# A feed-forward stage rebuilt: one batch through all eight experts, three batches by their two experts in 19 sorted tiles

## The chip, the core and the metric

The kernel runs on one core of a Trainium2 chip. The metric is the device time of one execution in microseconds. Five engines work beside each other, each on a list of its own: TensorE (PE in the profile, its weight loads PEld), VectorE (DVE), ScalarE (ACT), GpSimd (POOL) and SyncE (SP). SyncE here only starts transfers; ScalarE and GpSimd can start them too. An engine waits for another by a semaphore, and what stands behind a waiting instruction on its engine waits with it.

## The reference

Four batches of 256 tokens with 128 features. First cross-attention to 1,601 keys a batch, then a mixture of eight experts, of which each token uses two.

```python
x = x + attention(layernorm(x), ctx, Wq, bq, Wk, bk, Wv, bv)
h = layernorm(x).reshape(1024, 128)
scores = softmax(h @ router_weight.T + router_bias)          # 8 experts
topk_w, topk_idx = top_k(scores, 2)
gu = einsum('th,ehn->ten', h, gate_up_proj) + gate_up_bias   # 8 x (128 -> 512)
gate, up = minimum(gu[..., :256], 7), clip(gu[..., 256:], -7, 7)
act = (up + 1) * gate * sigmoid(1.702 * gate)
down = einsum('tei,eih->teh', act, down_proj) + down_bias    # 8 x (256 -> 128)
x = x + (down[topk_idx] * topk_w).sum(axis=1)
```

All is float32. Products whose rounding would move the result are made of three matmuls in a faster format: each operand is split into a high and a low part, and high x high, high x low and low x high are summed (`three`, lines 941 to 946).

## The kernel before

The 1,024 tokens are eight tiles of 128 (two a batch). The attention handles one tile after another: scores against 1,601 keys in four chunks (12 matmuls), clipping and maximum on VectorE, one exponential over the row on ScalarE (L419), 13 transposes of the probabilities (L1025), 13 matmuls with the context (L1041). TensorE's list interleaves tile n+1's scores with tile n's transposes and sums. At the end of each batch come the value projection (L1054), the residual (L655), the second layer norm (L662 to L674, its inverse root on GpSimd, L287), the transposes of the normalised tokens (L1064) and the router (8 logits a token).

The feed-forward stage computes all eight experts for all tokens and weighs the results; the six experts that a token doesn't use have weight zero. It has 16 steps: a step is one expert for one half (512 tokens), in the order (expert 0, half 0), (1, 0), (0, 1), (1, 1), then the next pair of experts. In a step TensorE computes four banks of 128 hidden units by 512 tokens, three matmuls of 512 columns each (`gate_up`), and after that the down projection of an earlier step, 16 matmuls of 128 columns (`down`, L1147). ScalarE applies silu and relu with bias to the banks (L498, L504) and scales the down results by the router's weights (L524); VectorE clips and multiplies (L838, L847) and splits the weights of each expert in high and low (L774, L779); GpSimd adds a step's result to the residual (L350). The steps of experts 2 to 5 stand in a loop, the rest is written out. All hands off in fixed order by semaphores; there is no planner.

The expert weights lie in SBUF as one tensor, loaded once. What the tokens are routed to changes only the weights of the sum, never which work is done or where it is read from. Results go out in three transfers, the first half while the last steps run.

## Time and profile before

| | |
|---|---|
| median of 3 runs | 156.98 us (156.92 to 156.98) |
| the profiled execution | 156.96 us, of which 155.2 us from the first to the last instruction |
| TensorE's granted clock | 1.00 of full speed (2.4 GHz) in every slice |
| busy: TensorE, VectorE, ScalarE, GpSimd | 96%, 66%, 65%, 32% |
| attention, up to the last tile's sums | 0 to 74.5 us, with the first steps of the experts in its end |
| feed-forward alone | 75.8 to 152.5 us on TensorE |
| after the last matmul | 2.7 us |

A line of the profile names engine, line, operation, output<-inputs and size; "busy" is the time in which such instructions ran, and the mean is of one. Two matmuls in a row overlap: one of 395 ns starts 234 ns after the one before it. So what a row of matmuls costs is read from the starts, not from the means. The same holds for ScalarE where nothing is waited for.

### The profile page before, as it was taken

What the parts mean: (1) busy time and instruction counts of PE and PEld (TensorE: products, weight loads), DVE (VectorE), ACT (ScalarE), POOL (GpSimd) and SP (SyncE); (2) the same over time, 40 slices, a digit from 0 to 9 for tenths busy, and PEclk for the clock granted to TensorE, in tenths of its full rate; (3) what the DMA queues carried; (4) which work ended last, traced back from release to release, by engine and by line L of the source; (5) the groups of instructions that cost most, each with busy time, mean ns of one, the idle gap of its engine ahead of it and who ended that gap; (6) DMA issues with size and microseconds to landing.
All of it is one profiled execution on the core that took longest, in us unless ns stands there. A gap on an engine that the chain in (4) does not pass through costs nothing.

```text
span 155.2 us, 3023 instructions
## 1 busy us (share of the span) xinstructions
PE 149.2 (96%) x1004; PEld 136.0 (88%) x1004; DVE 103.2 (66%) x288; ACT 100.8 (65%) x205; POOL 49.8 (32%) x49
## 2 busy tenths in 40 slices
PE   7998799999999999999999999999999999999993
PEld 7988699999999999989988888788888888887892
DVE  0668958386859595963683899957654377552773
ACT  3183878657484736468866656957788677779450
POOL 1356529243505300210067643312333321233020
PEclk9999999999999999999999999999999999999999
DMA  4979999700000000000000000000000000000022
GB/s 116 371 292 404 388 401 384 225 1 4 0 2 0 4 0 0 4 0 2 0 0 4 0 0 0 0 4 0 2 0 0 0 0 0 0 4 0 4 68 68
DMA packets 5909, 10.69 MB, mean 69 GB/s; under 512 B 380, under 2 KB 3080, under 8 KB 5896
## 3 DMA queue, kind: packets, MB, share of 16 engines
q1 hardware_dynamic: 4968, 10.00, 17.9%
q10 hardware_dynamic: 928, 0.53, 1.2%
...
q14 instruction: 6, 0.05, 0.1%
HBM read 10.00 MB, written 0.52 MB: 68 GB/s over the span
## 4 chain that ended last, share of the span: by engine, by line
PE 78%; DVE 10%; POOL 4%; ACT 3%; issue 3%; DVEq 0%
PE T L1147 14%; PE O L1041 13%; PE S L944 11%; PE S L946 10%; PE S L945 10%; PE T L1025 6%; PE S L951 3%; POOL ex L309 2%; DVE xT L847 2%; DVE up L838 1%; PE S L1147 1%; DVE w_lo L779 1%; DVE sc L631 1%; ACT pr L419 1%; POOL rstd L287 1%
## 5 line engine op out<-in xcount | busy, mean ns | idle before, releaser
L838 DVE TENSOR_SCALAR up<-up 128x512 f32<-128x512 f32 x32 | 13.9, 434 | 24.7 <-ACT up L504 24.7
L350 POOL TENSOR_TENSOR x<-x,xn 128x512 f32<-128x512 f32 x13 | 17.3, 1331 | 38.6 <-ACT xn L524 38.6
L427 ACT ACTIVATE pT<-T 128x512 f32<-128x512 f32 (+1 forms) x32 | 15.4, 513 | 18.4 <-PE T L1025 18.4
L524 ACT ACTIVATE xn<-T,w_scaled 128x128 f32<-128x128 f32 x56 | 16.1, 374 | 17.2 <-PE T L1147 14.1
L944 PE MATMUL S<-x_hi,w_hi 128*128 128x512 f32 x64 | 26.8, 419 | 0.2 <-DVE w_lo L779 0.2
L1041 PE MATMUL O<-pT,ctx_sb 128*128 128x128 f32 (+1 forms) x208 | 25.9, 275 | 0.2 <-ACT pT L427 0.2
L945 PE MATMUL S<-x_lo,w_hi 128*128 128x512 f32 x64 | 25.3, 395 | 0.0
L946 PE MATMUL S<-x_hi,w_lo 128*128 128x512 f32 x64 | 25.3, 395 | 0.0
L1041 PEld LDWEIGHTS O<-pT,ctx_sb 128*128 128x128 f32 (+1 forms) x208 | 24.6, 192 | 0.6 <-ACT pT L427 0.5
L631 DVE TENSOR_SCALAR_CACHE_REDUCE sc<-S,clip_hi 128x400 f32<-128x400 f32 (+1 forms) x32 | 18.9, 630 | 8.7 <-PE S L946 8.5
L498 ACT ACTIVATE keysT_sb<-S,gate_bias 128x512 f32<-128x512 f32 x32 | 22.7, 708 | 1.7 <-PE S L946 1.6
L504 ACT ACTIVATE up<-S,up_bias 128x512 f32<-128x512 f32 x32 | 22.5, 704 | 0.0
L287 POOL TENSOR_TENSOR rstd<-ve,minus_half 128x2 f32<-128x2 f32 (+1 forms) x7 | 7.5, 1076 | 36.7 <-DVE ve L674 27.6
L317 POOL TENSOR_TENSOR ct_lo<-keysT_sb,ct_hi 128x400 fp32r<-128x400 f32 (+1 forms) x12 | 12.5, 1060 | 14.0 <-ACT ct_hi L410 14.0
L1147 PEld LDWEIGHTS T<-dn_sb,xT 128*128 128x128 f32 x128 | 15.4, 192 | 0.9 <-issue 0.4
L1147 PE MATMUL T<-dn_sb,xT 128*128 128x128 f32 (+1 forms) x128 | 15.8, 276 | 0.2 <-DVE xT L847 0.2
L1025 PE MATMUL T<-ident,pr 128*128 128x128 f32 (+1 forms) x104 | 15.1, 274 | 0.6 <-ACT pr L419 0.6
L946 PEld LDWEIGHTS S<-x_hi,w_lo 128*128 128x128 f32 x64 | 12.0, 188 | 3.0
L1147 PEld LDWEIGHTS T<-dn_sb,act_odd 128*128 128x128 f32 x112 | 13.6, 191 | 1.0 <-DVE act_odd L847 0.4
L944 PEld LDWEIGHTS S<-x_hi,w_hi 128*128 128x128 f32 x64 | 12.1, 189 | 2.5 <-DVE w_lo L779 0.4
L1147 PE MATMUL T<-dn_sb,act_odd 128*128 (+1 forms) x112 | 14.0, 277 | 0.2 <-DVE act_odd L847 0.2
L945 PEld LDWEIGHTS S<-x_lo,w_hi 128*128 128x128 f32 x64 | 12.1, 189 | 2.1
(127 smaller groups left out, 248.4 us busy)
## 6 DMA issues: line engine op xcount, KB each, us to landing
...
ctx_sb<-in_ctx SPq DMA_DIRECT2D x3, 256.0 KB, 4.5
...
out_x<-xn SPq DMA_DIRECT2D x1, 256.0 KB, 2.3
out_x<-xn SPq DMA_DIRECT2D x2, 128.0 KB, 1.8
```

The source lines that it names most:

```text
L350: nc.gpsimd.tensor_tensor(acc, acc, y_sb[:, k % 2, :], ALU.add).then_inc(y_added, 1)
L498: nc.scalar.activation(gate[:, k % 2, ih, :], S[2 * ih][:], ACT.Silu, bias=gate_bias[:, bass.ds(col + ih, 1)], scale=ALPHA).then_inc(silu_ ...
L504: nc.scalar.activation(up[:, k % 2, ih, :], S[2 * ih + 1][:], ACT.Relu, bias=up_bias[:, bass.ds(col + 2 + ih, 1)]).then_inc(up_ready, 1)
L524: ins = nc.scalar.activation(y_sb[:, k % 2, t * DIM:(t + 1) * DIM], T[k % 2][:, t * DIM:(t + 1) * DIM], ACT.Copy, scale=w_scaled[:, bass.d ...
L631: nc.vector.tensor_scalar(sc[:, n % 2, c0:c0 + w], S[c][:, 0:w], clip_hi[:, n:n + 1], None, ALU.min, ALU.max, accum_out=row_max[:, n, c:c ...
L838: nc.vector.tensor_scalar(up[:, k % 2, ih, :], up[:, k % 2, ih, :], 2.0 * LIMIT, 1.0 - LIMIT, ALU.min, ALU.add).then_inc(up_clipped, 1)
L944: nc.tensor.matmul(dst, a_hi, b_hi, start=True, stop=False)
L945: nc.tensor.matmul(dst, a_hi, b_lo, start=False, stop=False)
L946: return nc.tensor.matmul(dst, a_lo, b_hi, start=False, stop=True)
L1025: ins = nc.tensor.transpose(T[bank][0:rows, (t - t0) * P:(t - t0 + 1) * P], pr[:, n % 2, t * P:t * P + rows], ident[:])
L1041: ins = nc.tensor.matmul(O[:, q * P:(q + 1) * P], ctx_sb[b][0:rows, t, :], pT[0:rows, t, :], start=(t == 0), stop=(t == KT - 1))
L1147: ins = nc.tensor.matmul(dst, act_t[k % 2][:, ih, t * P:(t + 1) * P], dn_sb[:, bass.ds((e * 2 + ih) * DIM, DIM)], start=(ih == 0), stop=(i ...
```

## The change

The attention stays. The feed-forward stage is another one:

- **Routing decides the work.** Batch 1 is still computed densely, all eight experts for its 256 tokens, in 16 dense steps of 128 hidden units (`dense_gate_up`, `dense_down`). Its work stands between the last attention tile and the first sorted tile.
- The 768 tokens of batches 0, 2 and 3 are sorted by expert. Each token's normalised row is copied twice (`copy_payload`), with its place in the result as 129th column. From the ranks of the logits VectorE finds the two experts; small matmuls (`count_before`) count how many rows go before each one; GpSimd computes the row numbers (`find_rows`) and scatters the rows by twelve indirect transfers of 128 rows (`send_rows`) into `slot_rows` in HBM, which one transfer of 3.6 MB has filled with ones before.
- VectorE computes a table of 19 tiles (12 full ones, and up to 7 more since each expert starts on a tile of its own): first row and expert of each. SyncE reads the first row of each tile from SBUF into a register and loads the tile from HBM. TensorE reads all 19 expert numbers into registers, in a row, after its first tile's transpose.
- A sorted tile is 128 rows of one expert: a transpose, a split, four matmuls of 512 columns (the bias by a matmul of its own, then three with the weights at the register's place), silu on ScalarE, clip and product on VectorE, two transposes, two matmuls of the down projection, and one indirect transfer from GpSimd that scatters the 128 results to `token_results` in HBM.
- When all 19 are there, they are loaded (256 KB a batch), weighed and added by VectorE, and sent out.
- All weights are split during the attention, in high parts by ScalarE (8 of 128x512) and low parts by GpSimd (6) and VectorE (2); they arrive in three transfers, in the space of the transposed keys.

The core of the diff:

```diff
+                e0, n = W_PARTS[k]
+                sp.wait_ge(keys_lo_ready, (k + 1) * NCH)
+                sp.dma_start(keysT_sb[:, k, 0:n * 2 * HIDDEN].rearrange("p (e n) -> p e n", e=n),
+                             gu[e0:e0 + n].rearrange("e h n -> h e n")).then_inc(w_in[k], 16)
...
+            def load_slots(i):
+                at = sp.value_load(first_row[0:1, i:i + 1], min_val=0, max_val=ROWS - P)
+                sp.dma_start(xt[:, i, :], xs[bass.ds(at, P), :]).then_inc(xt_in[i], 16)
...
+            sp.wait_ge(first_row_ready, 1)
+            for s in range(len(SPARSE)):
+                sp.wait_ge(rows_sent[s], 16 * TOP_K * TPB)
+            for i in range(SLOTS):
+                load_slots(i)
...
+            for place_of, count in sends():
+                sp.wait_ge(y_sent[place_of], count)
+            for s in (0, 2):
+                sp.dma_start(yb_sb[:, s], yb_v[:, s]).then_inc(yc_in[s], 16)
...
+            def send_rows(s, choices=range(TOP_K)):
+                pool.wait_ge(pads_in, 16)
...
+                for c in choices:
+                    for t in range(TPB):
+                        k = c * TPB + t
+                        nc.gpsimd.indirect_dma_start(xs[:, :], bass.IndirectOffsetOnAxis(ap=row_of[:, s, k:k + 1], axis=0),
+                                                     xp[:, SPARSE[s], c, t, :], None, bounds_check=ROWS - 1,
+                                                     oob_is_err=False).then_inc(rows_sent[s], 16)
+            def send_result(i):
+                pool.wait_ge(y_ready, i + 1)
+                nc.gpsimd.indirect_dma_start(yb[:, :], bass.IndirectOffsetOnAxis(ap=xt[:, i, DEST:DEST + 1].bitcast(I32), axis=0),
+                                             y_sb[:, i % Y_RING, :], None, bounds_check=TOP_K * RTOK - 1,
...
             root2(1)
+            weights_lo(3)
+            weights_lo(5)
+            find_rows(0)
+            send_rows(0, [0])
+            weights_lo(6)
+            weights_lo(7)
             root2(2)
+            copy_payload(2)
+            send_rows(0, [1])
+            find_rows(1)
...
+            send_rows(1)
+            copy_payload(3)
+            find_rows(2)
+            send_rows(2)
+            router_exponentials(3)
+            for i in range(SLOTS):
+                send_result(i)
+                if i < EXPERTS:
+                    add_dense(i)
...
-            def silus(step, k, col, ih):
-                act.wait_ge(gu_done, step * 4 + 2 * ih + 1)
-                if not isinstance(step, int) or step >= 2:
-                    act.wait_ge(act_ready, step * 2 + ih - 3)
-                nc.scalar.activation(gate[:, k % 2, ih, :], S[2 * ih][:], ACT.Silu, bias=gate_bias[:, bass.ds(col + ih, 1)],
-                                     scale=ALPHA).then_inc(silu_ready, 1)
...
+            def dense_silu(d):
+                act.wait_ge(d_done, d + 1)
+                if d >= 2:
+                    act.wait_ge(d_act_ready, d - 1)
+                e, ih = d // 2, d % 2
+                nc.scalar.activation(gate_d[:, d % 2, :], S[d % DENSE_RING][:, 0:QUERIES], ACT.Silu,
+                                     bias=gate_bias[:, e * 4 + ih:e * 4 + ih + 1], scale=ALPHA).then_inc(d_silu_ready, 1)
...
+            for d in range(DENSE_STEPS):
+                dense_silu(d)
+                dense_relu(d)
+                if d == 3:
+                    split_x2(last)
+                if d >= 4 and d % 2 == 0:
+                    dense_scale((d - 4) // 2)
+            dense_scale(EXPERTS - 2)
+            for k in range(-2, SLOTS + 2):
+                if 0 <= k - 2:
+                    evict(k - 2)
+                if 0 <= k - 1 < SLOTS:
+                    copy_act(k - 1)
+                if k + 2 < SLOTS:
+                    split_rows(k + 2)
+                if k == -2:
+                    dense_scale(EXPERTS - 1)
+                if 0 <= k + 1 < SLOTS:
+                    silu(k + 1)
+                if k in (BIAS_AT, BIAS_AT + 2):
...
+            for place_of, count in sends():
+                act.wait_ge(y_sent[place_of], count)
+            act.dma_start(yb_sb[:, 1], yb_v[:, 1]).then_inc(yc_in[1], 16)
...
                     split_x2(b)
-                    clip_scores(n + 1, [1, 2, 3])
+                    clip_scores(n + 1, [1, 2])
+                    clip_scores(n + 1, [3], counts=0 if n + 1 == 6 else None)
...
+            invert_sums(last)
...
+                if d == 4:
+                    add_router_bias(last)
+                    rank_experts(last)
+                if d == 5:
+                    add_regions(2)
+                    compare_counts()
+                if d == 8:
+                    tile_table()
+            for k in range(-2, SLOTS - 1):
+                if k + 2 < SLOTS:
+                    split_rows(k + 2)
+                if 0 <= k + 1:
+                    clip_up(k + 1)
+                    product(k + 1)
+                if k == 1:
+                    logit_maximum(last)
+                    logit_differences(last)
+                    expert_weights(1)
...
+            dve.wait_ge(bias_added, len(SPARSE))
+            for s in range(len(SPARSE)):
+                dve.wait_ge(yc_in[s], 16)
+                for t in range(TPB):
+                    first_sum(s, t)
+                for t in range(TPB):
+                    second_sum(s, t)
...
-            def gate_up(step, k, ih, loads):
-                _, h = PAIR_STEPS[k]
-                tok = slice(h * HTOK, (h + 1) * HTOK)
...
-                    if isinstance(step, int) and step == 0:
-                        if ih == 0 and part == 0:
-                            pe.wait_ge(s_free, TILES * NCH)
-                    else:
-                        pe.wait_ge(up_ready if part else silu_ready, step * 2 + ih - 1)
-                    col = slice((part * 2 + ih) * P, (part * 2 + ih + 1) * P)
-                    three(S[2 * ih + part][:], w_hi[buf][:, col], w_lo[buf][:, col], x2_hi[:, tok], x2_lo[:, tok]).then_inc(gu_done, 1)
...
-            def down(step, k, e, tiles_apart=False):
...
-                for t in range(HALF):
+                    pe.wait_ge(yd_scaled, e - 1)
+                if e == 0:
+                    pe.wait_ge(dn_in, 32)
+                pe.wait_ge(d_act_ready, 2 * e + 2)
...
-                            pe.wait_ge(act_ready, step * 2 + ih + 1)
-                        dst = S[t][:, 0:DIM] if tiles_apart else T[k % 2][:, t * DIM:(t + 1) * DIM]
-                        ins = nc.tensor.matmul(dst, act_t[k % 2][:, ih, t * P:(t + 1) * P],
-                                               dn_sb[:, bass.ds((e * 2 + ih) * DIM, DIM)], start=(ih == 0), stop=(ih == 1))
...
+            def dense_gate_up(d):
+                e, ih = d // 2, d % 2
...
                 for part in range(2):
...
+                    c = part * 2 + ih
+                    w = slice(e * P, (e + 1) * P)
+                    ins = three(S[d % DENSE_RING][:, part * QUERIES:(part + 1) * QUERIES], w_hi[:, c, w], w_lo[:, c, w],
+                                x2_hi[:, X2_PLACE[DENSE], :], x2_lo[:, X2_PLACE[DENSE], :])
+                ins.then_inc(d_done, 1)
...
+            def transpose_rows(i):
+                if i == 0:
+                    pe.wait_ge(d_relu_ready, DENSE_STEPS - 1)
+                else:
+                    pe.wait_ge(xt_lo_ready, i)
+                pe.wait_ge(xt_in[i], 16)
+                nc.tensor.transpose(XT_BANK[:, 0:P], xt[:, i, 0:DIM], ident[:]).then_inc(xt_done, 1)
+            def load_expert(i):
+                if i == 0:
+                    pe.wait_ge(table_ready, 1)
+                expert[i] = pe.value_load(expert_at[0:1, i:i + 1], min_val=0, max_val=(EXPERTS - 1) * P)
...
+                cols = bass.ds(expert[i], P)
+                dst = GU[i % 2][:].rearrange("p (c n) -> p c n", c=WIDTH)
+                nc.tensor.matmul(GU[i % 2][:], bias_pick[:, i:i + 1].to_broadcast([BIAS_ROWS, P]), bias_parts[:],
+                                 start=True, stop=False)
+                nc.tensor.matmul(dst, xt_hi[:, i % 2, :], w_hi[:, :, cols], start=False, stop=False)
+                nc.tensor.matmul(dst, xt_hi[:, i % 2, :], w_lo[:, :, cols], start=False, stop=False)
+                nc.tensor.matmul(dst, xt_lo[:, i % 2, :], w_hi[:, :, cols], start=False, stop=True).then_inc(gu_done, 1)
...
+                for c in range(2):
+                    ins = nc.tensor.matmul(T[i % 2][:, 0:DIM], act_t[:, i % 2, c, :], dn_sb[c][:, bass.ds(expert[i], DIM)],
+                                           start=(c == 0), stop=(c == 1))
+                ins.then_inc(y_done, 1)
...
+            for k in range(-2, SLOTS + 1):
+                if k + 2 < SLOTS:
+                    transpose_rows(k + 2)
+                if k == -2:
+                    dense_down(EXPERTS - 1)
+                    for i in range(SLOTS):
+                        load_expert(i)
+                if 0 <= k + 1 < SLOTS:
+                    gate_up(k + 1)
+                if 0 <= k - 1:
+                    down(k - 1)
+                if 0 <= k < SLOTS:
+                    transpose_act(k)
+                if k in (BIAS_AT, BIAS_AT + 2):
+                    transpose_weights((k - BIAS_AT) // 2)
+                if k in (BIAS_AT + 2, BIAS_AT + 4):
+                    routed_bias((k - BIAS_AT - 2) // 2)
 def kernel(x, ctx_1024, L0_xattn_Wq, L0_xattn_bq, L0_xattn_Wk, L0_xattn_bk, L0_xattn_Wv, L0_xattn_bv,
```

**TensorE, at the end of the attention.** In the kernel before, the first whole steps of 512 tokens and the first down projection (`T<-dn_sb`; S and T are PSUM banks, `x_hi` the tokens, `w_hi` the weights):

```order
L944 MATMUL S<-x_hi,w_hi 128x512 [waits silu_ready,w_ready]
L945 MATMUL S<-x_lo,w_hi 128x512
L946 MATMUL S<-x_hi,w_lo 128x512
L944 MATMUL S<-x_hi,w_hi 128x512 [waits up_ready]
...
L1147 MATMUL T<-dn_sb,act_odd 128x128 [waits act_ready,t_free1]
L1147 MATMUL T<-dn_sb,act_odd 128x128 [waits act_ready]
L1147 MATMUL T<-dn_sb,act_odd 128x128 x6
```

In the changed kernel, the dense steps of batch 1, with the router of batch 3 and its count between them:

```order
L1264 MATMUL S<-x_hi,w_hi 128x256 [waits d_relu_ready]
L1265 MATMUL S<-x_lo,w_hi 128x256
L1266 MATMUL S<-x_hi,w_lo 128x256
...
L1264 MATMUL M<-wr_hi,x_hi 128x8 [waits x2_lo_ready]
...
L1407 MATMUL O<-chosen,later_r 128x16 [waits chosen_ready,x1_ready,route_consts]
...
L1497 MATMUL T<-dn_sb,sc 128x128 [waits d_act_ready,yd_scaled]
```

Columns are halved, a step waits for the relu of four steps before, and the routing chain of batch 3 runs through this list.

**TensorE, from dense to sorted work.** The kernel before has no such place. In the changed one (`pr` holds the loaded rows, `expert_at` the table):

```order
L1510 MATMUL S<-ident,pr 128x128 [waits xt_in0,d_relu_ready]
L1497 MATMUL T<-dn_sb,sc 128x128 [waits d_act_ready,yd_scaled]
L1516 TENSOR_LOAD expert_at [waits table_ready]
L1516 ISA x2
...
L1510 MATMUL S<-ident,pr 128x128 [waits xt_in1,xt_lo_ready]
L1529 MATMUL S<-bias_parts,bias_pick 128x512 [waits d_relu_ready,xt_lo_ready,bias_ready]
L1531 ISA
L1531 MATMUL S<-w_hi,xt_hi 128x512
L1532 REGISTER_ALU
L1532 MATMUL S<-w_lo,xt_hi 128x512
```

The pair of the third and fourth row stands there 19 times. It is behind the transpose that waits for the first tile's transfer, and ahead of the first tile's matmuls.

**GpSimd.** Before, its list is the additions; the first of them, behind the router's powers:

```order
L317 TENSOR_TENSOR ct_lo<-keysT_sb,ct_hi 128x402
L287 TENSOR_TENSOR rstd<-ve,minus_half 128x2 [waits var2_ready] x3
L309 TENSOR_TENSOR ex<-e_base,logit 128x16 [waits ldiff_ready] x2
L350 TENSOR_TENSOR x<-x,xn 128x512 [waits y_scaled]
L350 TENSOR_TENSOR x<-x,xn 128x512 [waits y_added,y_scaled] x3
```

Now (batch 3's rows, then the first result):

```order
L406 TENSOR_TENSOR rstd<-ve,minus_half 128x2 [waits var2_ready]
L508 DMA slot_rows<-xp,row_of 7040x129 [waits row_ready,payload_copied,pads_in]
L508 DMA slot_rows<-xp,row_of 7040x129 x3
L481 COPY xp<-xp 128x2x128 [waits xn2_ready]
L488 TENSOR_TENSOR rows_of<-mask,place 128x32 [waits mask_ready,place_ready]
...
L497 CAST row_of<-rows 128x4 [waits row_steps]
...
L454 TENSOR_TENSOR ex<-e_base,ldiff 128x16 [waits ldiff_ready]
L515 DMA token_results<-pT,pr 1536x128 [waits y_ready]
L525 TENSOR_TENSOR x<-x,sc 128x256 [waits yd_scaled]
```

It issues 31 indirect transfers, 12 before the first sorted tile and one after each tile.

## Rows read from the trace of the kernel before

**Rows 1.** The page's head: span; busy time, share and instructions of an engine.

```profile
span 155.2 us, 3023 instructions
PE 149.2 (96%) x1004; PEld 136.0 (88%) x1004; DVE 103.2 (66%) x288; ACT 100.8 (65%) x205; POOL 49.8 (32%) x49
```

**Rows 2.** Busy time by stretch: us, each engine with count, clock, DMA share, GB/s.

```profile
100.00:110.00 10.00, 9.81 (x59) 8.45 (x59) 6.09 (x11) 7.21 (x18) 2.80 (x3) 1.00 0.01 2
150.00:155.20 5.20, 2.51 (x21) 2.17 (x19) 2.88 (x9) 0.00 (x0) 0.00 (x0) 1.00 0.24 71
```

**Rows 3.** Groups by line and shape: busy us, mean ns, idle before and its releaser.

```profile
L944 PE MATMUL S<-x_hi,w_hi 128*128 128x512 f32 x64 | 26.8, 419 | 0.2 <-DVE w_lo L779 0.2
L350 POOL TENSOR_TENSOR x<-x,xn 128x512 f32<-128x512 f32 x13 | 17.3, 1331 | 38.6 <-ACT xn L524 38.6
L498 ACT ACTIVATE keysT_sb<-S,gate_bias 128x512 f32<-128x512 f32 x32 | 22.7, 708 | 1.7 <-PE S L946 1.6
L524 ACT ACTIVATE xn<-T,w_scaled 128x128 f32<-128x128 f32 x56 | 16.1, 374 | 17.2 <-PE T L1147 14.1 <-DVE w_scaled L767 3.2
L838 DVE TENSOR_SCALAR up<-up 128x512 f32<-128x512 f32 x32 | 13.9, 434 | 24.7 <-ACT up L504 24.7
L847 DVE SCALAR_TENSOR_TENSOR xT<-keysT_sb,up 128x512 f32<-128x512 f32 x16 | 12.2, 763 | 0.6
L1147 PE MATMUL T<-dn_sb,xT 128*128 128x128 f32 x64 | 7.8, 275 | 0.0
L440 ACT ACTIVATE x_hi<-M 128x256 fp32r<-128x256 f32 x4 | 1.5, 379 | 1.3 <-PE M L1064 1.3
```

**Rows 4.** TensorE in order of time: start, us, what.

```profile
75.09 0.25 PE L946 MATMUL M<-wr_hi,x_lo 128*128 128x8 f32 x1
75.34 0.68 PE L1054 MATMUL O<-more_sb,oT 128*128 128x128 f32 x4
...
76.10 0.40 PE L945 MATMUL S<-x_lo,w_hi 128*128 128x512 f32 x1
76.34 0.40 PE L946 MATMUL S<-x_hi,w_lo 128*128 128x512 f32 x1
```

**Rows 5.** The chain that ended last: start, us, what.

```profile
110.31 1.78 PE T L1147 x16
...
150.50 2.03 PE S L1147 x16
152.62 0.35 DVE xn L936
```

**Rows 6.** ScalarE in order of time, idle before it in brackets.

```profile
62.92 0.60 ACT L427 ACTIVATE pT<-T 128x512 f32<-128x512 f32 x1 [1.99 <-PE T L1025]
...
70.69 1.28 ACT L532 ACT_TABLE_LOAD   x1
```

**Rows 7.** VectorE in order of time, batch 3's residual and variance.

```profile
76.13 0.61 DVE L655 SCALAR_TENSOR_TENSOR x<-O,inv_sum,xb 128x128 f32<-128x128 f32 x2 [0.34 <-PE O L1054]
...
77.58 0.17 DVE L674 TENSOR_SCALAR ve<-mv 128x2 f32<-128x2 f32 x1
```

**Rows 8.** Groups by line and shape, small operations.

```profile
L309 POOL TENSOR_TENSOR ex<-e_base,logit 128x16 f32<-128x16 f32 x2 | 5.9, 2959 | 2.2 <-DVE logit L703 2.2
L287 POOL TENSOR_TENSOR rstd<-ve,minus_half 128x2 f32<-128x2 f32 x5 | 5.8, 1165 | 31.2 <-DVE ve L674 27.6 <-DVE ve L587 3.6
L763 DVE TENSOR_REDUCE rank<-beats 128x32 f32<-128x256 f32 x2 | 0.8, 418 | 0.0
L295 POOL TENSOR_TENSOR shift<-neg_mean,rstd 128x3 f32<-128x3 f32 x2 | 0.4, 196 | 0.2
```

**Rows 9.** Transfers issued: what, queue, count, KB each, median us from issue to landing.

```profile
out_x<-xn SPq DMA_DIRECT2D x1, 256.0 KB, 2.3
out_x<-xn SPq DMA_DIRECT2D x2, 128.0 KB, 1.8
```

**Rows 10.** The chain of waits at the loop's start: start, us, what.

```profile
96.07 0.80 issue
```

885 lines of the change are left out of this document (559 added, 326 removed).

## The prediction

> **What bounds the kernel now.** I read the page's head first: TensorE is busy for 149.2 of 155.2 us, no other engine above 66% [rows 1]. Busy is an average, so the table by stretch comes next. Inside the feed-forward stage TensorE is at 10.00 of 10.00 us, at full clock, while ScalarE has 7.2 and VectorE 6.1; only the last 5 us are less full [rows 2]. The timeline then gives the price of TensorE's work, from start to start: 0.234 us for a matmul of 512 columns (76.10 to 76.34) [rows 4], 0.111 us for one of 128 columns (16 in 1.78) [rows 5]. The groups confirm the counts: three forms of 64 with 512 columns, 256 of the down projection, the 64 shown being a quarter [rows 3]. So 192 x 0.234 = 44.9 and 256 x 0.111 = 28.4, together 73.3 us of the 77.2 between the start of the value projection of batch 3 (75.34) [rows 4] and the end of the last matmul (152.53) [rows 5]. The bound is TensorE's work in the feed-forward stage. The end is short: the last VectorE instruction stops at 152.97 [rows 5], and 2.2 us later the last transfer of 128 KB (1.8 us) is in [rows 9].
>
> **What is removed and added on TensorE.** A matmul of 256 columns is not in the trace at these places; between 0.111 (128 columns) and 0.234 (512) I take half of the latter, 0.117. Dense: 16 steps x 6 = 96 x 0.117 = 11.2, and 32 x 0.111 = 3.6. A sorted tile: 4 x 0.234 + 5 x 0.111 (three transposes, two down) = 1.49, 19 of them 28.3. Sum 43.1 against 73.3: TensorE has 30.2 us less to do. If it stayed the bound, the time would be near 127. It doesn't: the new stage has a chain of routing, scatter and load in its middle and a chain of scatter, load and sum at its end. I follow these in absolute times of the profiled execution.
>
> **Attention.** The added work there goes by engine. ScalarE: eight copies of 128x512, about 0.6 each as L427, two at a time, so 1.2 us in gaps such as the 1.99 us ahead of that row [rows 6]. GpSimd: six splits near the 1.33 us of its 128x512 addition [rows 3] and four scatters, against 32% busy [rows 1]. VectorE sheds splits. TensorE is full there and nothing late feeds it, so I take zero; two spots have no reserve, the inverse root of batch 2 behind GpSimd's splits, and the switch of the activation table (1.28 us) [rows 6], which now also waits for batch 2's logits. Two whole gate-up groups (2.8 us) leave the last attention tile, but that tile then waits for the exponential and for this table, so I count 0.7 of them as won: the sums of tile 7 end near 73.8 instead of 74.5, where the router of batch 2 starts now (75.09 is its last matmul) [rows 4]. With the first dense step (0.7) and the projection (0.44), batch 3's values are there at **74.9**.
>
> **Routing chain of batch 3.** Count 0.34 and region addition 0.17: 75.5. Residual to variance as before, 76.13 to 77.75 = 1.6 [rows 7]: 77.1. Inverse root 1.2 [rows 8]: 78.3. The normalised rows (0.6) stand on VectorE behind two dense steps (four operations of 0.25 to 0.4): 79.8. Transposes 0.22, splits on ScalarE 0.38 [rows 3] and VectorE 0.4, router 0.66, hops: 82.2. Bias and the seven ranking operations, at half the elements of the 418 ns row [rows 8] 0.25 each: 83.9. Count matmuls 0.8 and addition: **85.1**. GpSimd's five operations for the row numbers, 0.2 to 0.3 each [rows 8]: 86.6.
>
> **The scatters.** The trace has no transfer issued by GpSimd. What one occupies of it lies between 0.2 us, its shortest arithmetic row, and 3.0, its longest [rows 8]; I take 1.2, the inverse root, because rows are built by software for 128 partitions in each. Four for batch 3: 91.4; landing 2.0, between the 1.8 and 2.3 of the output transfers [rows 9]: 93.4. SyncE reads a register, issues, 2.1 to land: the first tile is in at **95.9**. The dense stage is ScalarE's: 32 operations of 256 elements near the 0.38 of L440 and 16 scalings at 0.27, the 374 ns of L524 less what overlaps in a row [rows 3], 16.5 us, plus a wait for batch 3's transposes. It ends near 97.4 with the last dense down projection.
>
> **The register reads.** 19 reads with their register operations stand on TensorE's list ahead of the first sorted matmul, and what is behind them (transpose 1, then all 19 tiles) waits. No row shows one. The bounds are nothing at all (0.05) and the longest wait in which an engine only handled its loop and registers, 0.80 [rows 10]. I take 0.25, nearer to the short one, since each is one word: 19 x 0.25 = 4.8, so the first gate-up begins at **102.2**. What the range keeps: 1.0 to 15.2 us.
>
> The Trainium skill (DMA: Bandwidth & Descriptors, section Latency and other measured facts) gives such a load from a tensor to a register a floor of about 600 ns. By it these 19 reads alone would be an estimated 11.4 us, and the time some 6.7 us above my forecast. No row here shows one.
>
> **The 19 tiles.** TensorE's own 1.49 us isn't the pace. After a tile's gate-up its silu (0.47), clip (0.4), product (0.43), halves of L498, L838 and L847 with their fixed part [rows 3], and hops (0.15) take 1.45 us, in which TensorE has only the next tile's gate-up and the small matmuls, and ScalarE has four operations of 0.25 to 0.47 a tile with a wait before each. VectorE's router weights and bias stand between tiles in six places. I take 1.82 a tile, 33.8 from the first gate-up to the end of the last: **136.1**. Bounds: 1.55 (28) and 2.3 (42). After its idle stretch of 5 us TensorE may come back at the lower clock; every stretch before shows 1.00 [rows 2], so that price isn't in the trace. At 1.2 GHz one tile's gate-up would take twice its 0.94; I add 0.9 once: **137.0**. GpSimd: 19 x 1.2 + 8 additions of 0.78 (half the elements of L350 [rows 3]) = 29 us in these 34, covered.
>
> **The end.** Silu to evicted result of the last tile 2.7: 139.7. GpSimd's wait and scatter 1.7, landing 2.0: 143.4. Reload of 256 KB 2.2 [rows 9]: 145.6. Twelve weighings of 0.345, as the 0.35 of L936 [rows 5]: 149.8. Output 2.2 as before: 152.0. That stands against 155.2, and the 1.76 us around the span (156.96 less 155.2) stays: **153.7**, against a profiled 156.96 and a median of 156.98, 2.1% faster. Of 30 us of work saved, some 27 go into two round trips, the reads, and tiles paced by three engines. The forecast's own range, with scatters of 0.8 to 1.6, reads of 0.1 to 0.4 and tiles of 1.7 to 1.9, is 149 to 158.
>
> **The rivals.**
>
> - *Register reads at 0.6 us or more.* 19 x 0.35 = 6.7, and 0.35 in SyncE's first read: 160.7, slower. It decides from 0.25 + 3.3/19 = 0.42 us a read. For it: the reads stand in a row, each followed by two dependent register instructions. Against: the 0.80 of [rows 10] is a whole loop entry. Chance 0.24.
> - *GpSimd sets the pace.* From (34 - 6.2)/19 = 1.45 us a scatter it cannot follow the tiles. At 2.0 it adds 3.2 before the first tile and needs 44 us for the stage: 168. For it: 31 scatters on an engine at 32%, whose addition of 128x512 already takes as long as a tile's share. Against: only the first eight tiles carry an addition. Chance 0.12.
> - *Everything short.* Reads at 0.1 (-2.9) and tiles at 1.55 (-4.9): 146, faster. For it: ScalarE overlaps operations that wait for nothing. Chance 0.20.
> - *The attention pays.* If the inverse root of batch 2 comes 3 us late, TensorE stands in a stretch that is full now: 157. Chance 0.04.
>
> **Numbers.** Forecast 0.40. A measurement can tell 0.2% (0.3 us) from no change. Faster: 0.32 of the forecast, 0.20 of the short case and a little of the rest, 0.54. Same 0.05. Slower 0.41: the reads, GpSimd, and the upper edge of the forecast. Range 145.5 to 166: it takes in the short case and the slow reads, and leaves out slow scatters.
>
> **What would show it.** In the profile after: TensorE near 43 us busy from 73.8 on, instead of full; its first tile's transpose near 96; the idle time between that and the first matmul with bias, divided by 19, is the read. Starts of L1529 1.8 apart. ScalarE's scattered results: the last 3 to 4 us before the reload. A stage whose tiles are spaced by GpSimd's transfers, or a wait over 1 us at batch 2's inverse root, would prove me wrong at those steps; a first tile later than 100 would say that the scatters or the routing chain are mis-sized.

## The result and the profile after

The changed kernel takes 185.0 us in its profiled execution (span 183.0), against a forecast of 153.7 and a range that ended at 166. A second execution took 185.37 us. Some executions of the kernels with sorted tiles ran at a lower granted clock for longer (two of this one took 191.7 and 192.8 us); they are left out of the ratios and of the ranges, except where the text names them. The ratio to the kernel before (156.95) is 1.180 (95% interval 1.177 to 1.183). The page's head and two of its rows, which answer to [rows 1]; a digit is the busy share, in tenths, of a slice of 4.6 us; PEclk is TensorE's granted clock in tenths:

```profile
span 183.0 us, 3237 instructions
PE 144.9 (79%) x936; PEld 126.6 (69%) x936; DVE 107.9 (59%) x358; ACT 90.9 (50%) x218; POOL 82.6 (45%) x113
...
PE   6998999999989994996995930089979999998100
PEclk9999999999999998599999995555899999999955
```

TensorE's row shows zeros in its 25th and 26th slice, from 110 to 119 us: the array stands still. The clock is at 0.5 in the 17th slice, near 73 us, and from the 25th to the 28th, 110 to 128 us. I follow the prediction's milestones.

**Attention ends 6.6 us late.** VectorE, then TensorE, in order of time (start, duration, what, idle before and its releaser):

```profile
66.62 2.68 DVE L917 TENSOR_SCALAR ve<-mv 128x2 f32<-128x2 f32 x1
...
70.88 0.60 DVE L929 TENSOR_SCALAR xp<-x,mv,rstd 128x128 f32<-128x128 f32 x2 [0.62 <-POOL rstd L406]
```

```profile
71.54 0.44 PE L1384 MATMUL M<-ident,xp 128*128 128x128 f32 x2 [2.43 <-DVE xp L929]
72.07 1.97 PE L1345 MATMUL T<-ident,pr 128*128 128x128 f32 x8
```

And GpSimd beside them:

```profile
64.21 1.26 POOL L508 DMA_INDIRECT slot_rows<-xp,row_of  x1 [3.52 <-issue]
65.77 0.97 POOL L508 DMA_INDIRECT slot_rows<-xp,row_of  x1 [0.30 <-issue]
66.76 2.51 POOL L475 TENSOR_TENSOR w_lo<-keysT_sb,w_hi 128x512 fp32r<-128x512 f32 x2
69.38 1.46 POOL L406 TENSOR_TENSOR rstd<-ve,minus_half 128x2 f32<-128x2 f32 x1
```

The variance of batch 2, two numbers a partition, takes 2.68 us instead of 0.17 [rows 7]: it ends when GpSimd's two splits end. The inverse root waits behind both. TensorE idles 2.43 us, which is the wait of over 1 us at this place that the prediction named as a sign of being wrong. From 72 us on its matmuls start 0.20 to 0.21 us apart instead of 0.11: the clock is 1.2 GHz until 78.7.

**The reads idle the array for 0.62 us each.** TensorE between its first sorted tile's transpose and the first gate-up, and the instructions of the read's line by kind (duration min/median/max in ns, first and last start):

```profile
105.36 0.27 PE L1510 MATMUL S<-ident,pr 128*128 128x128 f32 x1
106.71 1.13 PE L1497 MATMUL T<-dn_sb,sc 128*128 128x128 f32 x8 [1.08 <-DVE sc L1158]
119.57 0.45 PE L1510 MATMUL S<-ident,pr 128*128 128x128 f32 x1 [11.73 <-issue]
119.95 0.79 PE L1529 MATMUL S<-bias_parts,bias_pick 16*128 16x512 f32 x1
```

```profile
L1516 PEldq TENSOR_LOAD <-expert_at x19: 293/301/493, 106.7 to 118.8; - x19
L1516 PEldq FUSED_REGOPS  x19: 146/146/165, 107.3 to 119.2; - x19
```

11.73 us of idle array for 19 reads are 0.62 each. The price of one is a little more, since the first read, begun at 106.7, ran beside the last eight rows of the dense stage: the loads' starts, 106.7 to 118.8, are 0.67 us apart. The load's own 301 ns is only half of that; its two register instructions and the steps between make the rest.

**The tiles.** By stretch (the columns are those of [rows 2]): the array's idle stretch, the first three tiles, the other sixteen.

```profile
105.36:119.95 14.59, 1.78 (x13) 1.19 (x11) 0.94 (x3) 1.72 (x7) 0.00 (x0) 0.64 0.25 59
119.95:129.19 9.24, 9.24 (x24) 5.85 (x23) 3.32 (x10) 2.53 (x9) 0.00 (x0) 0.50 0.15 36
129.19:165.93 36.74, 35.48 (x190) 25.84 (x189) 22.54 (x68) 18.36 (x62) 24.12 (x24) 0.99 0.07 24
```

The first three tiles run at 0.50 and are 2.5 to 3.8 us apart. After that TensorE is at 0.99 and busy 97% of the time, so it, and none of the three engines I had reckoned with, sets the pace. One tile at full clock, matmuls and weight loads (a row x4 or x2 merges as many):

```profile
141.67 0.18 PEld L1529 LDWEIGHTS S<-bias_parts,bias_pick 16*128 16x128 f32 x1 [0.17 <-issue]
141.67 0.49 PE L1529 MATMUL S<-bias_parts,bias_pick 16*128 16x512 f32 x1
142.09 0.19 PEld L1531 LDWEIGHTS S<-w_hi,xt_hi 128*128 128x128 f32 x1 [0.24 <-issue]
142.09 0.50 PE L1531 MATMUL S<-w_hi,xt_hi 128*128 x1
142.20 0.19 PEld L1532 LDWEIGHTS S<-w_lo,xt_hi 128*128 128x128 f32 x1
142.43 0.40 PE L1532 MATMUL S<-w_lo,xt_hi 128*128 x1
142.43 0.19 PEld L1533 LDWEIGHTS S<-w_hi,xt_lo 128*128 128x128 f32 x1
142.67 0.39 PE L1533 MATMUL S<-w_hi,xt_lo 128*128 x1
...
142.90 0.61 PE L1553 MATMUL T<-dn_sb,x_sb 128*128 x4
143.34 0.38 PE L1542 MATMUL S<-ident,x_sb 128*128 128x128 f32 x2
143.56 0.27 PE L1510 MATMUL S<-ident,pr 128*128 128x128 f32 x1
143.76 0.50 PE L1529 MATMUL S<-bias_parts,bias_pick 16*128 16x512 f32 x1
```

The starts are 2.09 us apart: 0.42 + 0.34 + 0.24 + 0.23 for the gate-up, 0.44 for the down projection, 0.22 and 0.20 for the transposes. The two places where the gate-up costs more than 0.234 [rows 4] are those around the bias matmul, whose weights are 16 rows high: there the weight load and its matmul start together, elsewhere the load stands beside the matmul before. What that costs a tile in all is measured below, in the experiment on the bias rows.

**The end** is near the forecast. The last scatter, the reload, the first weighing and the last:

```profile
171.97 0.97 POOL L515 DMA_INDIRECT token_results<-pT,pr  x1 [0.59 <-issue]
174.19 0.93 SPq L388 DMA_DIRECT2D keysT_sb<-token_results  x2
...
177.53 0.61 DVE L1196 SCALAR_TENSOR_TENSOR x<-keysT_sb,weight,x 128x128 f32<-128x128 f32 x2 [8.87 <-DMA keysT_sb<-token_results]
...
180.16 0.60 DVE L1202 SCALAR_TENSOR_TENSOR xn<-keysT_sb,weight,x 128x128 f32<-128x128 f32 x2
```

### The profile page after: what moved, and what is told of

Same layout as the page of the kernel before. It is cut to its first block, busy times and chain, and to the rows that moved or that the text cites. A ratio compares the mean times of both kernels' runs of the same rounds, so it can differ in the third digit from the quotient of the medians.

```text
span 183.0 us, 3237 instructions
## 1 busy us (share of the span) xinstructions
PE 144.9 (79%) x936; PEld 126.6 (69%) x936; DVE 107.9 (59%) x358; ACT 90.9 (50%) x218; POOL 82.6 (45%) x113
## 4 chain that ended last, share of the span: by engine, by line
PE 60%; DVE 16%; issue 12%; ACT 4%; DMA 3%; POOL 3%; DVEq 0%; POOLq 0%; ACTq 0%; SPq 0%
PE O L1361 9%; PE T L1345 5%; PE S L1529 5%; PE S L1531 5%; PE T L1553 4%; PE S L1264 4%; PE S L1266 3%; PE S L1265 3%; PE T L1497 3%; PE S L1271 3%; PE S L1533 3%; PE S L1532 3%; DVE sc L874 2%; PE S L1542 2%; DMA keysT_sb<-token_results 2%
## 5 line engine op out<-in xcount | busy, mean ns | idle before, releaser
L515 POOL DMA_INDIRECT token_results<-pT,pr x19 | 18.7, 982 | 15.3 <-ACT pT L767 12.8
L1169 DVE TENSOR_SCALAR xT<-S 128x256 f32<-128x256 f32 x19 | 8.0, 422 | 17.0 <-ACT xT L753 17.0
L753 ACT ACTIVATE xT<-S 128x256 f32<-128x256 f32 x19 | 7.3, 385 | 20.5 <-PE S L1533 20.5
L1510 PE MATMUL S<-ident,pr 128*128 128x128 f32 x19 | 6.0, 317 | 13.0 <-issue 11.7
L508 POOL DMA_INDIRECT slot_rows<-xp,row_of x12 | 12.6, 1048 | 7.4 <-issue 6.4
L624 ACT ACTIVATE pr<-sc,neg_max 128x1601 f32<-128x1601 f32 x8 | 13.0, 1630 | 2.9 <-DVE sc L883 2.9
L1345 PEld LDWEIGHTS T<-ident,pr 128*128 128x128 f32 (+1 forms) x104 | 13.3, 152 | 1.4 <-ACT pr L624 1.1
L1553 PEld LDWEIGHTS T<-dn_sb,x_sb 128*128 128x128 f32 x76 | 11.7, 198 | 3.5 <-issue 2.0
L1553 PE MATMUL T<-dn_sb,x_sb 128*128 x76 | 12.2, 285 | 1.3 <-ACT x_sb L759 1.3
L1264 PE MATMUL S<-ct_hi,g_hi 128*128 128x400 f32 (+1 forms) x32 | 12.4, 389 | 0.4 <-POOL ct_lo L528 0.4
L1497 PE MATMUL T<-dn_sb,sc 128*128 128x128 f32 x64 | 8.9, 282 | 4.7 <-DVE sc L1158 4.7
```

The lines of the kernel that those rows point to most:

```text
L508: nc.gpsimd.indirect_dma_start(xs[:, :], bass.IndirectOffsetOnAxis(ap=row_of[:, s, k:k + 1], axis=0), xp[:, SPARSE[s], c, t, :], None, bou ...
L515: nc.gpsimd.indirect_dma_start(yb[:, :], bass.IndirectOffsetOnAxis(ap=xt[:, i, DEST:DEST + 1].bitcast(I32), axis=0), y_sb[:, i % Y_RING, : ...
L624: nc.scalar.activation(pr[:, n % 2, 0:KEYS], sc[:, n % 2, 0:KEYS], ACT.Exp, bias=neg_max[:, n:n + 1], accum_out=row_sum[:, n:n + 1]).then_ ...
L1264: nc.tensor.matmul(dst, a_hi, b_hi, start=True, stop=False)
L1345: ins = nc.tensor.transpose(T[bank][0:rows, (t - t0) * P:(t - t0 + 1) * P], pr[:, n % 2, t * P:t * P + rows], ident[:])
L1497: ins = nc.tensor.matmul(T[e % 2][:, t * DIM:(t + 1) * DIM], act_d[:, (2 * e + ih) % DENSE_RING, t * P:(t + 1) * P], dn_sb[ih][:, e * DIM: ...
```

## The experiments

Line numbers move by a few lines between kernels. A `...` in an edit marks lines that are left out. Rows of a trace come from the profiled execution of that kernel, whose time is given where it lies outside the range. Executions differ by up to 1.4 us before any edit here has begun to act: VectorE's third variance (`ve`) starts at 22.58 us in the changed kernel and between 21.57 and 22.94 in the others.

### Twice the reads

```diff
                     for i in range(SLOTS):
                         load_expert(i)
+                    for i in range(SLOTS):
+                        load_expert(i)
```

> The 19 register reads stand twice in a row on TensorE's list (38 reads), the rest is the changed kernel. Theory A (each read, with its two register instructions, occupies TensorE's list for 0.62 us, none beside another): the idle time ahead of the first gate-up goes from 11.7 to 23.5 us, the time from 185.2 to 197. Rival B (the 11.7 us are one wait for something else, such as code being fetched or the table): the idle time stays near 12 us, the time within 1 us of 185.2. Rival C (reads overlap, the first one is dear): idle 12 to 15 us.

Measured: 199.4 to 202.1 us, and

```profile
130.66 0.45 PE L1510 MATMUL S<-ident,pr 128*128 128x128 f32 x1 [23.99 <-issue]
```

The 19 further reads added 12.26 us of idle time, 0.65 each: theory A. The first gate-up comes at 131.04 instead of 119.95. The time is 2 to 5 us above the 197 expected, because the half clock now holds for six tiles instead of three: the 19 tiles take 49.4 us from first to last start, against 46.0.

### No reads at all

```diff
-                expert[i] = pe.value_load(expert_at[0:1, i:i + 1], min_val=0, max_val=(EXPERTS - 1) * P)
+                expert[i] = i * EXPERTS // SLOTS * P
```

> The expert of each tile is a constant of the program (tile i takes expert i*8//19): no reads and no register arithmetic on TensorE; which expert's weights a tile meets is left out, every amount of work is the same. Theory A (reads 11.7 us in a row; the idle time brings the half clock for the first four tiles, some 8 us; register instructions between the matmuls stretch a tile from about 1.8 to 2.1 us): first gate-up near 108.5, clock 1.00 in the tiles, tiles 1.8 apart, time 185.2 - 11.7 - 8 - 5 = about 160. Rival B (the pace of 2.1 us is the matmuls' own or another engine's): the tiles stay at 2.1, time about 165. Rival C (the clock falls anyway, since the tiles leave TensorE too little to do): 0.50 for some tiles, time 168 to 174.

Measured: 171.0 to 173.4 us. The pace is rival B's, the time 6 us above its 165 (this kernel leaves out the routing's choice of weights, so its output is not the reference's). First gate-up 109.5, and tiles still 2.1 apart, with the same 0.42 and 0.34 us in them though no register instruction is left:

```profile
125.54 0.50 PE L1529 MATMUL S<-bias_parts,bias_pick 16*128 16x512 f32 x1
125.96 0.50 PE L1531 MATMUL S<-w_hi,xt_hi 128*128 128x512 f32 x1
126.30 0.40 PE L1532 MATMUL S<-w_lo,xt_hi 128*128 128x512 f32 x1
```

So addresses from registers cost nothing here, and my theory of stretched tiles fell. From the first to the last start the tiles take 42.3 us: without the idle stretch they are 3.7 us faster, not 8.

### One read a tile

```diff
-                    for i in range(SLOTS):
-                        load_expert(i)
+                    load_expert(0)
                 if 0 <= k + 1 < SLOTS:
                     gate_up(k + 1)
+                if 0 <= k + 2 < SLOTS and k + 2 > 0:
+                    load_expert(k + 2)
```

> Each expert number is read inside the tiles: that of tile 0 ahead of the first gate-up, that of tile i+1 right behind the four matmuls of tile i's gate-up; the rest is the changed kernel. Theory A1 (the read holds TensorE's sequencer only, and the matmuls queued ahead of it, 0.9 us of work, run on meanwhile): the idle time ahead of the first gate-up is about 1 us, tiles stay near 2.1 us, the clock near 1.00, time about 165 to 168. Theory A2 (a read stands between matmuls with its full 0.62 us): tiles 2.7 us apart, 11.2 us given back, but without the long idle time the clock stays up: time about 174 to 177. Rival B (the idle time isn't the reads): it stays near 11 us and the time near 185.

Measured: 170.7 and 171.3 us, on average 171.0, and, in two more executions, 175.5 and 175.8. First gate-up 109.86, tiles 2.09 apart, 41.85 us from first to last start: as good as no reads. The waits went as in A1; the time I gave it, 165 to 168, was 3 to 6 us too hopeful. The reads in a row cost 185.2 - 171.0 = 14.2 us: in the profiled executions 10.1 up to the first gate-up, and 4.1 in the tiles by the clock.

### Matmuls without a use between the reads

```diff
+                    pe.wait_ge(d_relu_ready, DENSE_STEPS - 3)
+                    pe.wait_ge(table_ready, 1)
                     for i in range(SLOTS):
+                        for _ in range(2):
+                            nc.tensor.matmul(S[0][:], ones_r[:], w_hi[:, :, 0:P], start=True, stop=True)
                         load_expert(i)
```

> The changed kernel with its 19 reads in a row, but two matmuls of 128x512 with no use ahead of each read. Theory A (the reads hold TensorE's sequencer, not its array; the clock falls because the array idles for 11.7 us): the matmuls run beside the reads, TensorE's stretch from its first transpose to the first gate-up stays near 13 us, the clock is 1.00 there and in the tiles, L1529's first start stays near 120 and its last comes 42 us later, as in e5, instead of 46: time about 181. Rival B (reads and matmuls don't overlap): the stretch grows by 38 x 0.23 = 8.9 us, the time to about 190. Rival C (the half clock comes from the tiles' own pattern): starts stay 2.5 to 3.8 us apart for the first three tiles, time 185.

Measured: 179.7 to 182.1 us, theory A. The stretch of reads and the tiles in this kernel (columns as above):

```profile
106.00:118.70 12.70, 12.62 (x41) 5.79 (x39) 0.00 (x0) 0.63 (x2) 0.00 (x0) 1.00 0.24 59
118.70:161.20 42.50, 40.65 (x213) 29.16 (x212) 26.43 (x78) 20.86 (x70) 24.95 (x24) 1.00 0.08 26
```

38 matmuls, 8.9 us of work, ran beside the reads: from the first read to the first gate-up it is 13.4 us (105.3 to 118.7) against 13.2 without them. The clock stayed at 1.00, and the tiles took 42.5 us instead of 46.0; over the four executions the mean clock was 0.95 to 0.96, against 0.86 to 0.90 in those of the changed kernel. So it was the idle array, and not the reads, that brought the half clock of the tiles, at 3.5 us here. Of the other 1.2 us by which this execution is ahead at the first gate-up, 1.0 stands already at 22 us.

### The two splits moved, three ways

GpSimd's splits for experts 6 and 7, first behind the inverse root of batch 2:

```diff
-            weights_lo(6)
-            weights_lo(7)
             root2(2)
             copy_payload(2)
+            weights_lo(6)
+            weights_lo(7)
```

> On GpSimd's list the low parts of the weights of experts 6 and 7 stand behind the inverse root and the copy of batch 2 instead of ahead of them; the rest is the changed kernel. Theory A (the first scatter, 3.5 us late, pushes the two splits onto VectorE's variance of batch 2, which takes 2.68 instead of 0.17 us beside them, and the root waits behind both; TensorE then idles 2.4 us and its clock halves for 6 us): the variance takes 0.17 us again, TensorE's wait ahead of the transposes of batch 2 falls below 0.3 us, the clock stays at 1.00, and the time is 185.2 - 2.4 - 3 = about 180. Rival B (the clock fell for another reason, such as the little work before it): the wait goes, the clock still falls, time about 182.8. Rival C (routing's end is set elsewhere, such as by GpSimd's scatters of batch 2): time above 184.

Measured: 181.7 to 183.6 us, about 2.8 less than the changed kernel (the profiled execution took 184.4). The variance is back at 0.17, but the wait only moved. GpSimd now has the splits at 68.93 to 71.47, and beside them stand two operations of VectorE's ranking, ahead of the low part of the tokens that the router needs:

```profile
69.15 1.20 DVE L971 TENSOR_TENSOR ties<-logit 128x128 f32<-128x128 f32 x1
70.38 1.23 DVE L972 TENSOR_TENSOR beats<-logit 128x128 f32<-128x128 f32 x1
...
72.20 0.27 PE L1264 MATMUL M<-wr_hi,x_hi 128*128 128x8 f32 x1 [2.03 <-DVE x_lo L935]
```

Then behind the two further scatters, on the kernel with one read a tile:

```diff
             root2(2)
             copy_payload(2)
             send_rows(0, [1])
+            weights_lo(6)
+            weights_lo(7)
...
-                    pe.wait_ge(w_lo_pool_ready, EXPERTS - 2)
+                    pe.wait_ge(w_lo_pool_ready, EXPERTS - 4)
...
```

> As e5_read_per_tile, but GpSimd's two low parts for experts 6 and 7 stand behind the two further scatters of the first part, in a stretch where both GpSimd and VectorE idle (the dense steps of experts 6 and 7 wait for them on their own). Theory A (VectorE's short operations wait behind a GpSimd operation of 1.25 us that runs at the same time, wherever it stands; in e4 the ties and beats took 1.20 us each instead of 0.29): variance of batch 2 0.17, ties and beats 0.29, TensorE's wait for the split of the router's operand below 0.3 us, clock of the last attention tile 1.00, first gate-up 5 to 6 us earlier than in e5, time about 165.5. Rival B (the wait for the activation table and the half clock remain, since the exponential of tile 7 ends late anyway): 168. Rival C: the dense steps wait for the splits instead; time 170 or more.

Measured: 167.3 to 168.2 us, 3.3 below the 171.0, which is rival B's time (the profiled execution took 173.4, with the half clock for 10 us of its tiles, from 122 us on). The variance is at 0.17 and the ranking at 0.29 an operation. GpSimd starts the splits at 71.69, and this time VectorE's logit differences take 2.68 us beside them; ScalarE's last exponential and the table switch stand behind those, TensorE behind ScalarE:

```profile
71.57 2.68 DVE L954 TENSOR_TENSOR ldiff<-logit,lmax 128x16 f32<-128x16 f32 x1
...
76.55 1.60 PE L1361 MATMUL O<-pT,ctx_sb 128*128 128x128 f32 x10 [3.00 <-ACT pT L632]
```

So these exponentials were given to GpSimd, behind its last scatter of rows (the other edits of the last kernel stay):

```diff
-            router_exponentials(last - 1)
             nc.scalar.activation(table_switch[:], minus_half[:, 0:1], ACT.Silu)
...
             send_rows(2)
+            router_exponentials(2)
             router_exponentials(3)
...
-                if b < BATCHES - 1:
+                if b < 2:
...
```

> As e7_splits_in_idle, but the exponentials of batch 2 are computed by GpSimd behind its last scatter of rows, so ScalarE's switch of the table doesn't wait for batch 2's logits. Theory A (in e7 TensorE waits 3.00 us in the sums of tile 7 for copies that stand behind ScalarE's exponential, 3.4 us of wait for VectorE's differences, and the 1.28 us of table): that wait falls below 0.5 us, the clock stays 1.00, first gate-up about 2.5 us earlier, time 165. Rival B (the chain of batch 3 is bound elsewhere before the first tile): the wait goes and the time stays at 167.5.

Measured: 165.9, 169.7, 170.7 and, profiled, 172.2 us. TensorE's 3.00 us of wait in the attention are gone and the first gate-up comes at 103.74, 3.1 us before the 106.83 of the last kernel (0.3 of it stands already at 22 us); but in the profiled execution the first six tiles then ran at 0.50, though no wait above 1.33 us stood in the 9 us ahead of them. The mechanism of A is shown, its gain in time only by the one execution of 165.9.

In these three places VectorE's small operations took 1.20 to 2.68 us beside a split, and 0.17 to 0.29 where the splits stood elsewhere. The Trainium skill (SBUF — State Buffer, section Who interferes with whom) has a rule that bears on all three: VectorE and GpSimd share a pair of ports, and where VectorE's operation has two inputs in SBUF or runs in a two-port mode, whoever issues first holds the pair for its whole instruction. The traces agree that an operation is held up for a whole split or two. Who was first they don't show that way: in the changed kernel the variance's record starts at 66.62, 0.14 us before the first split's, and it still ends behind both.

### An earlier scatter

```diff
             weights_lo(3)
+            pool.wait_ge(pads_in, 16)
+            nc.gpsimd.indirect_dma_start(xs[:, :], bass.IndirectOffsetOnAxis(ap=xp[:, 0, 0, 0, DEST:DEST + 1].bitcast(I32), axis=0),
+                                         ones[:, 0:ROW], None, bounds_check=ROWS - 1, oob_is_err=False).then_inc(rows_sent[0], 16)
             weights_lo(5)
             find_rows(0)
+            pool.wait_ge(rows_sent[0], 16)
             send_rows(0, [0])
```

> As e5_read_per_tile, with one more scatter (128 rows of ones, where ones are) on GpSimd about 9 us ahead of the first real one. Theory A (the first indirect transfer of an execution costs GpSimd 3.3 us once, before it starts): the 3.3 us stand ahead of the added scatter, the idle time ahead of the first real one falls to 0.3 to 0.9 us, time within 2 us of e5. Rival B (the 3.3 us are a wait of the first real scatter for something of its own, such as the row numbers or the fill): it keeps its 3.3 us. Of the 3.3 us little is won in the end, since the added scatter pushes GpSimd's row numbers back by as much.

GpSimd from the added scatter to the inverse root of batch 2:

```profile
54.35 1.28 POOL L551 DMA_INDIRECT slot_rows<-ones,xp  x1 [0.19 <-issue]
56.55 1.09 POOL L475 TENSOR_TENSOR w_lo<-keysT_sb,w_hi 128x512 fp32r<-128x512 f32 x1 [0.92 <-ACT w_hi L656]
...
61.84 1.04 POOL L508 DMA_INDIRECT slot_rows<-xp,row_of  x1 [0.91 <-POOL row_of L497]
...
64.18 2.52 POOL L475 TENSOR_TENSOR w_lo<-keysT_sb,w_hi 128x512 fp32r<-128x512 f32 x2
67.11 1.46 POOL L406 TENSOR_TENSOR rstd<-ve,minus_half 128x2 f32<-128x2 f32 x1 [0.41 <-DVE ve L921]
```

The 3.3 us of idle GpSimd are at neither place, so neither theory came out as written, but A isn't refuted. GpSimd's queue handles the added scatter's register move at 51.6, 2.7 us before the scatter starts, and an inverse root and a split run in between; in the changed kernel the first scatter's move is at 60.8, 3.4 us before its start, with nothing in between. A price paid once, and hidden here beside that work, would look like this. Another candidate: an 8 KB transfer of instructions falls into the idle stretch of the changed kernel (62.2) and comes at 57.8 here. Neither was tested, and what the 3.3 us are stays open.

That they matter is shown: without them the splits end before the variance, which takes 0.17 us, TensorE's wait of 2.31 us goes, the clock stays at 1.00 up to 90 us, and the first gate-up comes at 105.27 instead of 109.86. Measured: 163.2, 166.1, 171.5 and 176.1 us. The profiled execution is the one of 166.1; it is 4.5 us below the profiled 170.7 of the kernel with one read a tile, and the tiles of the two take the same 41.8 us, so the gain lies ahead of them.

### The bias over 128 rows

```diff
-BIAS_ROWS = 2 * EXPERTS
+BIAS_ROWS = 128
...
-        "in_ffn_bias": a(np.tile(np.asarray(L0_ffn_gate_up_bias), (2, 1))),
+        "in_ffn_bias": a(np.tile(np.asarray(L0_ffn_gate_up_bias), (BIAS_ROWS // EXPERTS, 1))),
```

> As e5_read_per_tile, but the bias matmul of a tile contracts over 128 rows (the 16 rows of bias and 112 more with a zero factor) instead of 16. Theory A (in the 2.10 us of a tile, 0.19 us lies behind the 16-row matmul and 0.11 us behind the next one, because the weights of a matmul of another height aren't loaded while the one before runs; register instructions have nothing to do with it): starts of L1529 about 1.78 apart where no other work stands between, idle of weight loads ahead of L1531 gone, time 5 to 6 us below e5's 170.9. Rival B (the 0.42 us from L1529 to L1531 are the price of changing banks or of the moving operand's pattern): the tiles stay at 2.10 and the time within 1 us of e5's. Rival C (another engine takes over the pace, VectorE with 1.3 us a tile or the chain silu to transposed product): tiles 1.9 to 2.0.

Measured: 163.9 to 165.8 us, 1.049 (1.043 to 1.056) of the kernel before, about 6 below 171.0. The profiled execution took 166.4, 4.3 below the profiled 170.7; its tiles take 37.8 us from first to last start instead of 41.85, so 4.1 us are shown to be the edit's. One tile:

```profile
126.39 0.19 PEld L1529 LDWEIGHTS S<-bias_parts,bias_pick 128*128 128x128 f32 x1
126.42 0.48 PE L1529 MATMUL S<-bias_parts,bias_pick 128*128 128x512 f32 x1
126.50 0.19 PEld L1531 LDWEIGHTS S<-w_hi,xt_hi 128*128 128x128 f32 x1
126.74 0.39 PE L1531 MATMUL S<-w_hi,xt_hi 128*128 x1
...
128.11 0.48 PE L1529 MATMUL S<-bias_parts,bias_pick 128*128 128x512 f32 x1
```

1.69 us a tile instead of 2.09: theory A. It equals 4 x 0.234 + 7 x 0.111 = 1.71. So the 16-row matmul cost 0.40 us a tile: the starts ahead of it, behind it and behind the next matmul are now 0.17, 0.10 and 0.11 us closer. Of 18 x 0.40 = 7.2 us the kernel got 4.1, since VectorE doesn't keep up everywhere: TensorE's waits for it in the tiles grew from 0.26 and 0.98 us to 0.51 and 1.81.

### The bias work at the end, and all together

```diff
...
-                if k in (BIAS_AT, BIAS_AT + 2):
-                    transpose_weights((k - BIAS_AT) // 2)
-                if k in (BIAS_AT + 2, BIAS_AT + 4):
-                    routed_bias((k - BIAS_AT - 2) // 2)
+            transpose_weights(0)
+            transpose_weights(1)
+            routed_bias(0)
+            routed_bias(1)
...
```

> As e5_read_per_tile, but the transposes of the routing weights, the down bias's matmuls and its addition stand behind the last tile, in the time in which the last results are scattered and reloaded, and the weights of the three sparse batches are computed two tiles apart instead of one. Theory A (TensorE sets the pace of the tiles, so what it does beside them costs its full time: four tiles in which starts are 0.43, 1.67 and 1.23 us further apart, and 0.98 us of waiting at VectorE's weights): last gate-up 4 us earlier, time about 167. Rival B (GpSimd's scatters, 1.93 us apart with additions, then set the pace or the end): last scatter less than 1.5 us earlier, time 169.5. Rival C (the work moved to the end outlasts the reload): VectorE's sums start later than the reload lands, time 170 or more.

Measured: 164.6 to 166.4 us, 5.6 below the 171.0, more than the 4 expected. From first to last start the tiles take 39.2 us instead of 41.85; the other 3 us or so come from ahead of the tiles, where this execution is 4.1 earlier (first gate-up 105.71). The edit touches nothing there: 1.2 of the 4.1 stand already at 22 us, and TensorE's clock between 74 and 82 us was 0.84 instead of 0.67. So I count 2.7 for the edit.

> All of it at once: reads inside the tiles, bias matmul over 128 rows, the two splits in the idle stretch, bias work at the end. If the terms add: 170.9 - 5.5 - 5.4 - 4 = 156, level with the kernel before (156.9). If a next engine takes over in the tiles (VectorE with its three operations a tile and the weights, or GpSimd at 1.93 us a scatter with addition): tiles 1.9 to 2.0 apart and about 159 to 161.

Measured: 160.4 to 161.1 us, 1.027 (1.025 to 1.029) of the kernel before: the time expected if a next engine takes over. Tiles are 1.70 apart in the second half, but VectorE's weights now cost waits of 0.49, 1.46 and 1.21 us, since a faster tile leaves it less room, and the wait of 3 us for ScalarE in the attention is there as well (2.98).

> e9_all_four with four more edits: the exponentials of batch 2 on GpSimd instead of ScalarE, so that the switch of the activation table doesn't wait for the logits; the routing weights of batches 1 and 0 in VectorE's idle stretch ahead of the last residual; those of batches 2 and 3 one small step a tile; at the end the reload is issued ahead of batch 1's output. If the terms add: 160.4 - 2.5 (table) - 3.1 (waits at VectorE's weights in the tiles: 0.49 + 1.46 + 1.21) - 0.5 (reload) = 154.3, 1.6% below the kernel before (156.8). Rival B (the scatters of batch 3 and their chain set the first gate-up, so what attention and the dense stage give is lost): 156 to 157. Rival C (GpSimd, which now computes one batch's powers more and collides with VectorE, sets the tiles' pace): 158 or more.

Measured: 154.6, 154.7, 155.9 and 156.3 us against 156.85, a ratio of 0.990 (0.986 to 0.995): faster than the kernel before by 0.5 to 1.5%, the only version here that is, and between the 154.3 of the terms added up and rival B. First gate-up 104.38, last 136.44, two waits at VectorE of 0.45 and 0.56 us, weighings from 148.51 us on. In this profiled execution (155.9 us) TensorE is busy for 131.7 of 154.0 us.

## Why the prediction was wrong

The forecast was 2% faster, the measurement is 18% slower. The prediction's frame held: work saved on TensorE, given back to two round trips and the reads, and the sums at the end. The 31.3 us of error, by its milestones, in the profiled execution:

| step | forecast | measured | error added |
|---|---|---|---|
| values of batch 3 there | 74.9 | 81.5 | 6.6 |
| last place of batch 3 | 85.1 | 92.9 | 1.2 |
| row numbers, scatters, first tile in (measured: its transpose) | 95.9 | 105.3 | 1.6 |
| first gate-up | 102.2 | 119.95 | 8.3 |
| end of the last gate-up | 137.0 | 167.2 | 12.5 |
| output, with what lies around the span | 153.7 | 185.0 | 1.1 |

- **"Nothing late feeds it, so I take zero" (attention), 6.6 us.** I named the spot, the inverse root of batch 2 behind GpSimd's splits, and gave it a chance of 0.04, at 157 us. The mechanism was another than queueing alone: the splits also stopped VectorE's variance (2.68 us instead of 0.17), and behind the 2.43 us of idle TensorE the clock fell to 1.2 GHz for 6.8 us. GpSimd's new work was weighed by its share of the span, 32% [rows 1], and not by what stands beside it at that moment. Shown by the edits there: the added scatter brings the first gate-up 4.6 us forward (0.1 of it there at 22 us already); the moved splits 3.0 (0.9 there already), and the exponentials on GpSimd 3.1 more (0.3). Because this step came first, the prediction's own sign, that a first tile later than 100 would mean mis-sized scatters or routing, would have misled: those two were 2.8 us off together, and this one 6.6.
- **"I take 0.25, nearer to the short one" (reads), 6.9 us, and 4.1 more through the clock.** In the prediction's terms, idle time over 19, the value was 0.62, the size of the rival at 0.6, which had the mechanism right. The Trainium skill's floor of about 600 ns (DMA: Bandwidth & Descriptors, section Latency and other measured facts) agrees in size with the 0.65 to 0.67 from one read to the next. The choice was made from rows that don't resemble the operation. The rest of the 8.3, 1.4 us: the dense stage ended 2.5 us behind the first tile's transpose (107.8 less 105.3) and not 1.5, and 0.4 is the second tile's transpose, which stands between the reads and the first gate-up.
- **"I add 0.9 once" (clock).** It was 4.1, over three tiles and not one: 3.2 us more. The mechanism was right: with matmuls between the reads the clock stayed at 1.00 and the tiles took 3.5 us less.
- **"TensorE's own 1.49 us isn't the pace", 1.82 a tile.** It is the pace, at 2.10. The 1.49 was too small by 0.61. Of that 0.22 is the count: the trace writes a down projection matmul as two rows of 0.111, so two of them are four rows, as the sixteen rows of [rows 5] are eight instructions, and the sum is 1.71; the same slip made 3.6 out of the dense stage's 7.1, without effect. The other 0.4 is the 16-row bias matmul, as its 128 rows show. Against the 1.82 of the forecast it is 0.28 a tile, 19 x 0.28 = 5.3 us.
- **"VectorE's router weights and bias stand between tiles in six places."** They were taken as covered. On the engine that sets the pace they cost 2.7 us (bias work), and the waits for VectorE 1.3 (0.35 and 0.91). With the 3.2 and the 5.3 that is the 12.5.
- **Scatters and the end** were right within 20%: 0.97 us busy and 0.30 beside it, 1.27 a scatter instead of 1.2, and 17.8 us from the last gate-up to the output instead of 16.7.

Even with reads at no price the changed kernel would have been at 171, slower than before: no single step decided the sign.
